# Attention between two feed-forward passes: the probability tile of each head's longest query tile transposed by DMA, and norm, loads and waits moved at the change of sequence

## Chip, cores and metric

One NeuronCore of a Trainium2 chip runs the whole program. The metric is the device time of one execution in microseconds (us); before the change it is 3945.35, the median of three runs (3943.01 to 3945.7). A difference of 0.2% is about 8 us.

## What is computed

`x` holds 8 sequences of 1024 tokens with 256 values each. Three stages follow one another, each with a layer norm ahead and a residual behind it:

```python
x = x + 0.5 * ffn(layernorm(x), w_gate, w_up, w_down)        # inputs and weights rounded blockwise to FP4
x = x + attention(layernorm(x), Wq, Wk, Wv, Wo, span_val)
x = x + 0.5 * ffn(layernorm(x), w_gate, w_up, w_down)
# attention: 16 heads of 64
w = einsum('bhqd,bhkd->bhqk', q, k) / 64 + causal            # -1e9 above the diagonal
w = softmax(w) * mask                                        # mask: one value per head and key
w = w / (sum(w) + 1e-8)
out = einsum('bhqk,bhkd->bhqd', w, v) @ Wo
```

Only the attention stage is touched, apart from the way the split weights are stored for it.

## The kernel before

**Pairs and visits.** The attention stage works on two heads at a time, a pair: 8 pairs per sequence, 64 in all. A pair goes through 16 *visits* (`UNITS`), one for each head and query tile of 128 rows, for each head in the order of tiles `ORDER = (7, 0, 5, 1, 6, 3, 4, 2)`. Because of the causal mask, tile j meets only the j+1 first key tiles. So visit 0 and visit 8 are the long ones: tile 7 of either head, 1024 keys wide.

**One visit.** TensorE computes the scores into one of two banks `s_ps` (L1121 to L1125). VectorE takes the row maximum (`at_neg_max`, L1298). ScalarE writes the exponentials to `at_e_rows`, with the row sum, which costs a second short instruction (L1215). The value product needs the keys on the partitions, so TensorE transposes `e_rows` in blocks of 128x128 float32 into one of two banks `t_ps` (L1135), in *groups* of up to four blocks (512 columns). ScalarE copies each group as the f16 high part (`at_eT_hi`, L1223), VectorE the f16 rest (`at_eT_lo`, L1304). TensorE multiplies both with the values into `o_ps` (L1149), ScalarE copies the result out (`at_o_raw`, L1231). There is one bank `o_ps`: the first product of a visit waits for the copy of the visit before.

**Side work.** Beside the visits runs the work for the next pair and the last one, in *pieces* that share one bank `at_side_ps`: two pieces each for q and k of the next pair, four for v of the next two pairs (in every second pair, called odd here; the others are the even ones), two transposes of the last pair's output (`o_turn`) and four products with Wo. A piece of q, k or `o_turn` is done when ScalarE has copied the high part (L1195) and VectorE the rest (L1266); only then may the next piece enter the bank. In the last pair of a sequence (the fresh pair) there are four more pieces that transpose the next sequence's normed input (`x_turn`).

**Order.** Every engine is in order. The order is written out by `pair_steps`, which gives TensorE, ScalarE and VectorE one list: scores run two visits ahead, a group's value product three groups behind its transposes (`LAG`), and a piece stands behind the group whose number `SLOTS` (or `FRESH_SLOTS`) names. The high and the low copy of a piece stand one place later in the list than the piece. The steps are `scores`, `turn` (transposes and high copy), `lo`, `max`, `value`, `copy`, `exp`, and the pieces. Semaphores carry the dependencies.

**Change of sequence.** The fresh pair begins on VectorE with the whole norm of the next sequence (`norm_x`: 8 statistics, 8 aggregations, a power on GpSimd, 8 normalisations) and TensorE's first `x_turn` waits for it. SyncE's queue issues all loads in program order: in the first pair of a sequence it loads the next x, stores the accumulator `at_acc` once the last products of the former sequence are added, loads it anew, and only then, in the next pair's part, loads `at_w_qk` for the pair after.

## Time and profile before

| | |
|---|---|
| median of three runs | 3945.35 us |
| the profiled execution | 3950.1 us, of which the span from first to last instruction 3948.3 us |
| mean granted TensorE clock | 0.962 of 2.4 GHz |
| busy share of the span | TensorE 89%, VectorE 76%, ScalarE 60%, GpSimd 21% |
| attention stage | about 600 to 3420 us of the span, 64 pairs |

How to read it: the busy shares are means over three stages. Inside the attention stage, the timeline rows have the start of an instruction in us from the span's start, its duration, the engine, the line of the kernel, the output and inputs, and the shapes. A matmul's duration is from start to finished result, and matmuls overlap; what one costs TensorE is the distance to the start of the next. In brackets stands how long the engine was idle before and what ended that.

### The profile page before, as it was taken

The numbers are of one execution on the slowest core, as the hardware profiler recorded it, in microseconds if no ns is written. First come the engines' busy times: TensorE is split into PE (matmuls) and PEld (weight loads), VectorE is DVE, ScalarE is ACT, GpSimd is POOL, SyncE is SP. The second block draws the span as 40 slices with busy tenths as digits, with TensorE's granted clock in tenths as the row PEclk, the third lists the DMA queues.
The fourth block names the chain that finished last, engine by engine and source line by source line (L and its number), as shares of the span: only waits on it lengthen the run. The fifth ranks groups of instructions, "written<-read, shape, count | busy, mean of one in ns | idle before, by whom it ended". The sixth has DMA issues, their size and how long they took to land. (4 is left out here: it accounts for less than half of the span.)

```text
span 3948.3 us, 90120 instructions
## 1 busy us (share of the span) xinstructions
PE 3531.2 (89%) x29924; PEld 3175.8 (80%) x29924; DVE 3005.0 (76%) x4884; ACT 2363.7 (60%) x5622; POOL 819.8 (21%) x830
## 2 busy tenths in 40 slices
PE   0899996998999899889988988998898899599998
PEld 0899995887787788778877877887787788499998
DVE  7899974777677677767766776777777677599996
ACT  1455543776676577667766766676676667445544
POOL 2232321111121121112111111121111112122332
PEclk6999998999999999999999999999999999799999
DMA  6111114533543444344444534353443534211110
GB/s 205 52 57 56 50 35 128 118 94 86 129 120 86 119 105 107 86 119 109 108 100 107 121 89 119 93 124 83 123 100 90 129 86 111 103 36 57 48 56 33
DMA packets 160297, 372.56 MB, mean 94 GB/s; under 512 B 19552, under 2 KB 59360, under 8 KB 159456
## 3 DMA queue, kind: packets, MB, share of 16 engines
q1 hardware_dynamic: 159968, 368.73, 36.1%
q8 instruction: 139, 2.28, 0.2%
q14 instruction: 190, 1.56, 0.1%
HBM read 128.79 MB, written 38.54 MB: 42 GB/s over the span
## 5 line engine op out<-in xcount | busy, mean ns | idle before, releaser
L1223 ACT ACTIVATE at_eT_hi<-at_t_ps 128x512 f16<-128x512 f32 (+3 forms) x1536 | 744.7, 491 | 565.5 <-PE at_t_ps L1135 520.3
L1304 DVE SCALAR_TENSOR_TENSOR at_eT_lo<-at_t_ps,at_eT_hi 128x512 f16<-128x512 f32 (+3 forms) x1536 | 824.7, 551 | 222.9 <-ACT at_eT_hi L1223 132.6
L1215 ACT ACTIVATE at_e_rows<-at_s_ps,at_neg_max 128x1024 f32<-128x1024 f32 (+7 forms) x1024 | 765.6, 748 | 111.0 <-DVE at_neg_max L1298 110.6
L1135 PE MATMUL at_t_ps<-at_ident,at_e_rows 128*128 128x128 f32 x4608 | 786.1, 280 | 33.0 <-DVE at_eT_lo L1304 29.2
L1298 DVE TENSOR_REDUCE at_neg_max<-at_s_ps 128x1 f32<-128x1024 f32 (+7 forms) x1024 | 766.5, 749 | 47.3 <-PE at_s_ps L1125 36.9
L1121 PE MATMUL at_s_ps<-at_kh_st,at_q_st 128*128 128x512 f32 (+2 forms) x1536 | 585.4, 381 | 54.6 <-ACT at_e_rows L1215 26.8
L1149 PE MATMUL at_o_ps<-at_v_cols,at_eT_hi 128*128 128x130 f16 x4608 | 611.2, 221 | 17.8 <-ACT at_o_raw L1231 16.2
L1149 PE MATMUL at_o_ps<-at_v_cols,at_eT_lo 128*128 128x65 f16 x4608 | 569.4, 193 | 0.0
L1135 PEld LDWEIGHTS at_t_ps<-at_ident,at_e_rows 128*128 128x128 f32 x4608 | 510.6, 142 | 70.3 <-DVE at_eT_lo L1304 46.9
L1122 PE MATMUL at_s_ps<-at_kl_st,at_q_st 128*128 128x512 f32 (+2 forms) x1536 | 518.3, 345 | 0.0
L1149 PEld LDWEIGHTS at_o_ps<-at_v_cols,at_eT_hi 128*128 128x128 f16 x4608 | 435.9, 98 | 34.4 <-ACT at_o_raw L1231 20.1
L1050 PE MATMUL at_side_ps<-at_xT_hi,at_w_qk 128*128 128x512 f32 x1012 | 390.8, 427 | 60.0 <-DMA at_w_qk<-w_qk_split 51.3
L1149 PEld LDWEIGHTS at_o_ps<-at_v_cols,at_eT_lo 128*128 128x128 f16 x4608 | 420.6, 98 | 16.7
L1121 PEld LDWEIGHTS at_s_ps<-at_kh_st,at_q_st 128*128 128x128 f32 x1536 | 293.3, 191 | 96.0 <-ACT at_e_rows L1215 38.7
L1014 POOL TENSOR_TENSOR at_o_sum<-at_o_raw 128x1040 f32<-128x1040 f32 x64 | 131.5, 2054 | 940.4 <-ACT at_o_raw L1231 940.4
L1122 PEld LDWEIGHTS at_s_ps<-at_kl_st,at_q_st 128*128 128x128 f32 x1536 | 294.8, 192 | 23.3
L425 POOL TENSOR_TENSOR ffn_h_q<-ffn_code,ffn_scale 128x704 f32<-128x704 f32 x128 | 175.4, 1391 | 585.8 <-DVE ffn_code L366 585.8
L1231 ACT ACTIVATE at_o_raw<-at_o_ps 128x130 f32<-128x130 f32 x1024 | 290.7, 284 | 2.1 <-PE at_o_ps L1149 1.6
L1050 PEld LDWEIGHTS at_side_ps<-at_xT_hi,at_w_qk 128*128 128x128 f32 x1012 | 196.6, 194 | 100.4 <-DMA at_w_qk<-w_qk_split 52.3
L530 PE MATMUL ffn_gu_ps<-ffn_w_gu_hi,ffn_xT_hi 128*128 128x352 f32 x1024 | 262.2, 337 | 14.5 <-DVE ffn_raw L329 10.0
L467 ACT ACTIVATE ffn_silu<-ffn_gu_ps 128x704 f32<-128x704 f32 x128 | 97.1, 759 | 282.6 <-PE ffn_gu_ps L530 282.6
L530 PE MATMUL ffn_gu_ps<-ffn_w_gu_lo,ffn_xT_hi 128*128 128x352 f32 x1024 | 250.4, 326 | 0.0
(184 smaller groups left out, 7402.2 us busy)
## 6 DMA issues: line engine op xcount, KB each, us to landing
at_kh_st<-at_k_hi SPq DMA_DIRECT2D x256, 256.0 KB, 4.4
at_kl_st<-at_k_lo SPq DMA_DIRECT2D x256, 256.0 KB, 5.8
at_w_qk<-w_qk_split SPq DMA_DIRECT2D x64, 512.0 KB, 6.1
at_q_st<-at_q_hi SPq DMA_DIRECT2D x128, 256.0 KB, 3.9
at_q_st<-at_q_lo SPq DMA_DIRECT2D x128, 256.0 KB, 4.9
at_w_v<-w_v_split SPq DMA_DIRECT2D x66, 256.0 KB, 5.7
at_w_out<-w_out_split SPq DMA_DIRECT2D x64, 256.0 KB, 5.7
ffn_x_rows<-in_L_attn_query_dram SPq DMA_DIRECT2D x32, 256.0 KB, 2.8
```

Source lines behind the costliest of these rows:

```text
L425: nc.gpsimd.tensor_tensor(blocks_of(h_q[:, par, j, :INNER]), blocks_of(code[:, j * INNER:(j + 1) * INNER]), per_block(scale[:, par, j * HB ...
L530: last = nc.tensor.matmul(gu_ps[:, c, 0:HALF_I], xT[a][:, par, kt, j * P:(j + 1) * P], gu[b][:, kt, c * HALF_I:(c + 1) * HALF_I], start=n ...
L1050: last = nc.tensor.matmul(bank[:], wts[:, w, s, kt, :], xT[t][:, kt, c * CHUNK:(c + 1) * CHUNK], start=i == 0, stop=i == len(passes) - 1)
L1121: nc.tensor.matmul(out, qs, kh_st[par][a][:, k0:k0 + w], start=True, stop=False)
L1122: last = nc.tensor.matmul(out, qs, kl_st[par][a][:, k0:k0 + w], start=False, stop=not lastc)
L1135: last = nc.tensor.transpose(t_ps[i % 2][:, b * P:(b + 1) * P], e_rows[:, n % 4, (k0 + b) * P:(k0 + b + 1) * P], ident[:])
L1149: last = nc.tensor.matmul(o_ps[:, :VPART[s]], eT[s][:, i % EBUF, b * P:(b + 1) * P], v_cols[par][:, k0 + b, a, :VPART[s]], start=k0 + b == ...
L1215: nc.scalar.activation(e_rows[:, n % 4, :w], s_ps[n % 2][:, col:col + w], ACT.Exp, bias=neg_max[:, n % 4:n % 4 + 1], accum_out=e_sum[:, pa ...
L1223: nc.scalar.activation(eT[0][:, i % EBUF, :count * P], t_ps[i % 2][:, :count * P], ACT.Copy, scale=PSCALE).then_inc(sem("eT_hi"), 1)
L1231: nc.scalar.activation(o_raw[:, a * QT + j, :], o_ps[:, :VCOLS], ACT.Copy).then_inc(sem("o_copied"), 1)
L1298: nc.vector.tensor_reduce(neg_max[:, n % 4:n % 4 + 1], s_ps[n % 2][:, col:col + P * (j + 1)], AX.X, ALU.max, negate=True).then_inc(sem("ma ...
L1304: nc.vector.scalar_tensor_tensor(out=eT[1][:, i % EBUF, :count * P], in0=t_ps[i % 2][:, :count * P], scalar=PSCALE, in1=eT[0][:, i % EBUF, ...
```

## The change

1. **Visits 0 and 8 (tile 7 of either head) get no `turn`.** Their two groups each leave the list `GROUPS` (24 groups become 20). Instead ScalarE copies the 1024 columns of `e_rows` as f16 high part into `e_flat` (`flat_hi`), right behind the visit's `exp`; VectorE writes the rest beside it (`flat_lo`), at the end of the visit before; SyncE issues one DMA transpose of 128 x 2048 f16 (512 KB) into `eT_flip`; and TensorE multiplies all eight blocks at once (`value_flip`), behind the last value group of the visit two further on (visit 2 or 10).
2. **The lists move**: `SLOTS`, `FRESH_SLOTS` and `NORM` are new, `max` stands at a visit's second place or where it has one only, `EBUF` is 5, the value product stays three groups behind, where groups are now fewer.
3. **Change of sequence**: `norm_x` goes in 14 steps into places 8 and up of the sequence's first pair, x is loaded at that pair's start, `at_w_qk` is loaded one pair earlier into the buffer that the pair has just used (two more pairs are stored in DRAM for that), and VectorE's wait for `at_acc` stands ahead of the first sum with Wo instead of at the pair's start.

```diff
+FLIPPED = (7,)
+FLIPS = [n for n, (a, j) in enumerate(UNITS) if j in FLIPPED]
+FLIP_AFTER = {n + 2: n for n in FLIPS}
-NORM = (7, 8)
-SLOTS = (0, 2, 4, 6, 8, 10, 11, 13, 15, 17, 19, 20, 21, 22)
+NORM = (6, 7)
+ROWS_FROM = 8
+SLOTS = (0, 1, 3, 5, 7, 9, 10, 11, 13, 15, 17, 18, 19, 20)
-EBUF = 6
+EBUF = 5
...
+    def values_of(i, dg):
+        steps.append(("value", i, dg))
+        m = GROUPS[i][0]
+        if LAST_GROUP[m] == i:
+            steps.append(("copy", m, dg))
+            if m in FLIP_AFTER:
+                steps.append(("value_flip", FLIP_AFTER[m], dg))
+                steps.append(("copy", FLIP_AFTER[m], dg))
...
-        for i in [i for i, (m, _, _) in enumerate(GROUPS) if m == n]:
-            first = GROUPS[i][1] == 0
+        for first, i in enumerate([i for i, (m, _, _) in enumerate(GROUPS) if m == n] or [None]):
+            place += 1
...
+            if rows and place >= ROWS_FROM:
+                steps.append(("norm_x", place - ROWS_FROM, 1))
...
+        if soon[0] in FLIPS and (soon[1] == 0 or after):
+            steps.append(("flat_lo",) + soon)
         if more:
             steps.append(("exp",) + unit)
+            if unit[0] in FLIPS:
+                steps.append(("flat_hi",) + unit)
...
+            def flip(f, g):
+                sp.wait_ge(sem("flat_lo"), g * len(FLIPS) + f + 1)
+                sp.sem_inc(sem("passed_sp"), 1)
+                sp.wait_ge(sem("value_done"), g * NV + (VALUES.index(("flip", FLIPS[f])) + 1 - NV + AHEAD["value_done"]))
+                sp.sem_inc(sem("passed_sp"), 1)
+                sp.dma_start_transpose(eT_flip[f][:], e_flat[f][:].rearrange("p s k -> p (s k)")).then_inc(sem(f"flipped{f}"), 16)
...
             def pair(b, r, par, before, after, fresh, twin):
                 g = b * PAIRS + r
+                flip(0, g)
+                if isinstance(r, int) and r == 0 and not (isinstance(b, int) and b == BATCH - 1):
+                    sp.wait_ge(sem("xn"), b * QT + QT)
+                    load_x(b + 1)
                 if after:
-                    if not (isinstance(g, int) and g == 0):
-                        sp.wait_ge(sem("k_done"), g * 2)
-                    load_qk(g + 1, 0 if fresh else r + 1, 1 - par)
+                    sp.wait_ge(sem("k_done"), g * 2 + 2)
+                    load_qk(r + 2, par)
                     place(g + 1, 1 - par)
+                flip(1, g)
...
+            def value_flip(n, g, par):
+                a, j = UNITS[n]
+                f = FLIPS.index(n)
+                pe.wait_ge(sem(f"flipped{f}"), g * 16 + 16)
+                pe.wait_ge(sem("o_copied"), g * NU + (COPIED.index(n) + AHEAD["o_copied"]))
+                for b in range(j + 1):
+                    for s in range(2):
+                        last = nc.tensor.matmul(o_ps[:, :VPART[s]], eT_flip[f][:, s * (j + 1) + b, :], v_cols[par][:, b, a, :VPART[s]],
+                                                start=b == 0 and s == 0, stop=b == j and s == 1)
+                last.then_inc(sem("value_done"), 1)
...
+            def flat_hi(n, g):
+                nc.scalar.activation(e_flat[f][:, 0, :], e_rows[:, n % 4, :w], ACT.Copy, scale=PSCALE).then_inc(sem("flat_hi"), 1)
...
+            def flat_lo(n, g):
+                nc.vector.scalar_tensor_tensor(out=e_flat[f][:, 1, :], in0=e_rows[:, n % 4, :w], scalar=PSCALE, in1=e_flat[f][:, 0, :],
+                                               op0=ALU.mult, op1=ALU.subtract).then_inc(sem("flat_lo"), 1)
```

What the list does to the engines is shown at three places. The lines of the changed kernel are numbered anew: L1181 is the old L1135 (transposes), L1195 the old L1149 (value products), L1167 to L1171 the scores.

**ScalarE, visit 7 to 8 of every pair.** Before, from visit 8's `exp` (1024 wide) to the high copy of the first `o_turn` piece and the first copy of a transposed group of visit 8:

```order
L1215 ACTIVATE at_e_rows,at_e_sum<-at_s_ps,at_neg_max 128x1024
...
L1223 ACTIVATE at_eT_hi<-at_t_ps 128x384
L1231 ACTIVATE at_o_raw<-at_o_ps 128x130
...
L1215 ACTIVATE at_e_rows,at_e_sum<-at_s_ps,at_neg_max 128x128
...
L1195 ACTIVATE at_oT_hi<-at_side_ps 128x512
...
L1223 ACTIVATE at_eT_hi<-at_t_ps 128x512
```

The same stretch now:

```order
L1278 ACTIVATE at_e_rows,at_e_sum<-at_s_ps,at_neg_max 128x1024
...
L1288 ACTIVATE at_e_flat<-at_e_rows 128x1024
...
L1296 ACTIVATE at_eT_hi<-at_t_ps 128x384
...
L1305 ACTIVATE at_o_raw<-at_o_ps 128x130
...
L1278 ACTIVATE at_e_rows,at_e_sum<-at_s_ps,at_neg_max 128x128
L1263 ISA
L1255 ACTIVATE at_oT_hi<-at_side_ps 128x512
L1278 ACTIVATE at_e_rows,at_e_sum<-at_s_ps,at_neg_max 128x768
L1255 ACTIVATE at_oT_hi<-at_side_ps 128x512
```

The copy to `e_flat` stands ahead of four instructions that other work waits for; the two 512-wide copies behind the first `oT_hi` are gone.

**TensorE, between the two `o_turn` pieces (visit 8).** Before, with repeated rows left out:

```order
L1089 MATMUL at_side_ps<-at_ident,at_o_norm 128x128 x4
...
L1125 MATMUL at_s_ps<-at_causal,at_ident_b 128x128
...
L1135 MATMUL at_t_ps<-at_ident,at_e_rows 128x128 x4
L1149 MATMUL at_o_ps<-at_v_cols,at_eT_hi 128x130
L1149 MATMUL at_o_ps<-at_v_cols,at_eT_lo 128x65
...
L1135 MATMUL at_t_ps<-at_ident,at_e_rows 128x128 x4
...
L1089 MATMUL at_side_ps<-at_ident,at_o_norm 128x128 x4
```

Now:

```order
L1135 MATMUL at_side_ps<-at_ident,at_o_norm 128x128 x4
...
L1167 MATMUL at_s_ps<-at_kh_st,at_q_st 128x512
L1168 MATMUL at_s_ps<-at_kl_st,at_q_st 128x512
L1167 MATMUL at_s_ps<-at_kh_st,at_q_st 128x256
L1168 MATMUL at_s_ps<-at_kl_st,at_q_st 128x256
L1171 MATMUL at_s_ps<-at_causal,at_ident_b 128x128
...
L1135 MATMUL at_side_ps<-at_ident,at_o_norm 128x128 x4
```

Between the two pieces only the scores are left; eight transposes and ten value products went (the products to later places).

**TensorE, between the two q pieces at a pair's start (visits 0 and 1).** Before, from the last product of the first q piece to the first of the second:

```order
L1050 MATMUL at_side_ps<-at_xT_hi,at_w_qk 128x512
...
L1135 MATMUL at_t_ps<-at_ident,at_e_rows 128x128 x4
...
L1149 MATMUL at_o_ps<-at_v_cols,at_eT_hi 128x130
L1149 MATMUL at_o_ps<-at_v_cols,at_eT_lo 128x65
...
L1125 MATMUL at_s_ps<-at_causal,at_ident_b 128x128
...
L1135 MATMUL at_t_ps<-at_ident,at_e_rows 128x128
```

Now:

```order
L1096 MATMUL at_side_ps<-at_xT_hi,at_w_qk 128x512
...
L1167 MATMUL at_s_ps<-at_kh_st,at_q_st 128x256
L1168 MATMUL at_s_ps<-at_kl_st,at_q_st 128x256
L1171 MATMUL at_s_ps<-at_causal,at_ident_b 128x128
L1179 ISA
L1181 MATMUL at_t_ps<-at_ident,at_e_rows 128x128
L1195 MATMUL at_o_ps<-at_v_cols,at_eT_hi 128x130
L1195 MATMUL at_o_ps<-at_v_cols,at_eT_lo 128x65
```

A group of four transposes and the products that stood with it are gone from here, and ahead of the first piece another group of four and eight products are gone; one run of eight products follows the single transpose.

## Rows read from the trace of the kernel before

**Rows 1.** Windows: us of the stretch, busy us of each engine (instructions), clock, DMA, GB/s
```profile
700.00:800.00 100.00, 97.07 (x911) 85.31 (x910) 78.30 (x137) 71.84 (x196) 19.37 (x22) 1.00 0.47 113
```
**Rows 2.** TensorE's waits, 800 to 3200 us: sum us, times, longest us
```profile
PE at_side_ps L1050 <- DMA at_w_qk<-w_qk_split: 51.3, 7, 7.9
PE at_side_ps L1081 <- DVE at_xn L1330: 41.2, 7, 5.9
```
**Rows 3.** Windows of 5 us behind either wait at one change of sequence
```profile
935.00:940.00 5.00, 5.00 (x37) 4.45 (x37) 3.04 (x6) 3.23 (x9) 2.05 (x1) 0.67 0.01 3
1030.00:1035.00 5.00, 5.00 (x25) 3.96 (x24) 2.14 (x4) 2.26 (x6) 0.00 (x0) 0.61 0.00 0
```
**Rows 4.** Timeline of TensorE, visit 6 of an even pair
```profile
742.97 0.61 PE L1135 MATMUL at_t_ps<-at_ident,at_e_rows 128*128 128x128 f32 x4
743.41 0.22 PE L1149 MATMUL at_o_ps<-at_v_cols,at_eT_hi 128*128 128x130 f16 x1
...
743.76 0.30 PE L1135 MATMUL at_t_ps<-at_ident,at_e_rows 128*128 128x128 f32 x1
```
**Rows 5.** Groups by shape, 700 to 800 us: busy us, mean ns
```profile
L1223 ACT ACTIVATE at_eT_hi<-at_t_ps 128x512 f16<-128x512 f32 x30 | 17.9, 597 | 14.9 <-PE at_t_ps L1135 12.6 <-issue 2.2
L1223 ACT ACTIVATE at_eT_hi<-at_t_ps 128x384 f16<-128x384 f32 x10 | 4.9, 489 | 3.2 <-PE at_t_ps L1135 2.9
L1298 DVE TENSOR_REDUCE at_neg_max<-at_s_ps 128x1 f32<-128x1024 f32 x5 | 6.1, 1224 | 0.5 <-PE at_s_ps L1125 0.2
```
**Rows 6.** Timeline of ScalarE, visits 7 and 8, same pair
```profile
744.54 1.11 ACT L1215 ACTIVATE at_e_rows<-at_s_ps,at_neg_max 128x1024 f32<-128x1024 f32 x1
...
746.02 0.27 ACT L1231 ACTIVATE at_o_raw<-at_o_ps 128x130 f32<-128x130 f32 x1
...
746.52 0.61 ACT L1195 ACTIVATE at_oT_hi<-at_side_ps 128x512 fp32r<-128x512 f32 x1
...
749.13 0.90 ACT L1215 ACTIVATE at_e_rows<-at_s_ps,at_neg_max 128x768 f32<-128x768 f32 x1
```
**Rows 7.** Timeline of VectorE, the same stretch
```profile
747.16 0.69 DVE L1266 SCALAR_TENSOR_TENSOR at_oT_lo<-at_side_ps,at_oT_hi 128x512 fp32r<-128x512 f32 x1 [0.45 <-ACT at_oT_hi L1195]
747.76 0.95 DVE L1298 TENSOR_REDUCE at_neg_max<-at_s_ps 128x1 f32<-128x768 f32 x1
```
**Rows 8.** Timeline of TensorE, the same stretch
```profile
747.02 0.61 PE L1135 MATMUL at_t_ps<-at_ident,at_e_rows 128*128 128x128 f32 x4
...
748.37 0.63 PE L1089 MATMUL at_side_ps<-at_ident,at_o_norm 128*128 128x128 f32 x4
...
750.18 0.50 PE L1121 MATMUL at_s_ps<-at_kh_st,at_q_st 128*128 128x512 f32 x1 [0.23 <-ACT at_e_rows L1215]
```
**Rows 9.** Timeline of ScalarE at visit 7 of the next, odd pair
```profile
785.39 0.49 ACT L1223 ACTIVATE at_eT_hi<-at_t_ps 128x384 f16<-128x384 f32 x1 [0.76 <-PE at_t_ps L1135]
```
**Rows 10.** Timeline of TensorE and ScalarE around the start of that pair
```profile
762.19 1.11 ACT L1215 ACTIVATE at_e_rows<-at_s_ps,at_neg_max 128x1024 f32<-128x1024 f32 x1
...
764.33 0.23 PE L1125 MATMUL at_s_ps<-at_causal,at_ident_b 128*128 128x128 bf16 x1
...
765.19 0.48 PE L1050 MATMUL at_side_ps<-at_xT_hi,at_w_qk 128*128 128x512 f32 x1
...
766.67 0.60 PE L1135 MATMUL at_t_ps<-at_ident,at_e_rows 128*128 128x128 f32 x4
...
768.59 0.48 PE L1050 MATMUL at_side_ps<-at_xT_hi,at_w_qk 128*128 128x512 f32 x1
```
**Rows 11.** Timeline of VectorE in the fresh pair: the normalisation
```profile
929.48 2.67 DVE L1330 TENSOR_SCALAR at_xn<-at_x,at_moments,at_rstd 128x256 f32<-128x256 f32 x8 [1.77 <-POOL at_rstd L983]
```
**Rows 12.** DMA of the page: packets, MB, share of 16 engines; KB and us to landing
```profile
q1 hardware_dynamic: 159968, 368.73, 36.1%
...
at_kl_st<-at_k_lo SPq DMA_DIRECT2D x256, 256.0 KB, 5.8
at_w_qk<-w_qk_split SPq DMA_DIRECT2D x64, 512.0 KB, 6.1
```
**Rows 13.** SyncE's queue in that even pair, last placements of k
```profile
744.09 3.39 SPq L913 DMA_DIRECT2D at_kl_st<-at_k_lo  x4
```

More of the change, by code:

```diff
@@ L608 @@
 LAG = 3
-EBUF = 6
+EBUF = 5
+VALUES, COPIED = [], []
+for group, (unit, _, _) in enumerate(GROUPS):
+    VALUES.append(("group", group))
+    if LAST_GROUP[unit] == group:
+        COPIED.append(unit)
+        if unit in FLIP_AFTER:
+            VALUES.append(("flip", FLIP_AFTER[unit]))
+            COPIED.append(FLIP_AFTER[unit])
+NV = len(VALUES)
 def score_chunks(j):
@@ L619, in score_chunks, with starts_rows, pair_steps @@
     return [(CHUNK - first, 0, first), (CHUNK, first, w - first)]
-def pair_steps(before, after, fresh, values):
+def starts_rows(b, r):
+    return isinstance(r, int) and r == 0 and not (isinstance(b, int) and b == BATCH - 1)
+def pair_steps(before, after, fresh, values, rows=False):
     q, k, v, turn_o, wo, turn_x = ([(kind, c, dg) for c in range(n)] for kind, n, dg in (
@@ L746, in stored @@
     def stored(sp):
-        for order, count in enumerate((128, 64, 64, 32)):
+        for order, count in enumerate((128, 128, 128, 32)):
             sp.wait_ge(sem(f"kept{order}"), count)
@@ L1167, in pair @@
                 prev = ("k_lo", 2 * g + 2)
-                for kind, i, dg in pair_steps(before, after, fresh, par == 1):
+                for kind, i, dg in pair_steps(before, after, fresh, par == 1, starts_rows(b, r)):
                     if kind == "scores":
@@ L1240, in pair @@
                 g = b * PAIRS + r
-                for kind, i, dg in pair_steps(before, after, fresh, par == 1):
+                for kind, i, dg in pair_steps(before, after, fresh, par == 1, starts_rows(b, r)):
                     if kind == "exp":
                         exp(i, g + dg, par ^ dg)
+                    elif kind == "flat_hi":
+                        flat_hi(i, g + dg)
                     elif kind == "turn":
```

145 lines of the change are left out of this document (84 added, 61 removed).

## The prediction, written before the changed kernel was run

> **What bounds the kernel now.** I read the windows first. In a stretch of the attention stage without a change of sequence TensorE is busy 97% at the full clock, VectorE 78%, ScalarE 72% [rows 1]: TensorE bounds it. Then its waits: apart from short ones there are two of 5.9 and 7.3 us, once per change of sequence [rows 2]: the first transpose of the new input waits for the norm, and a pair later the projection waits for its weights, which SyncE issues only after the accumulator's store and load. Behind either wait the granted clock is 0.67 and 0.61 for a while, between the levels 1.2 and 2.4 GHz, since TensorE had stood still [rows 3]. Last the timelines, for how much room TensorE's order leaves to the copies of the side bank. At visit 8 of an even pair the first `o_turn` piece's rest is done at 747.85 and TensorE asks for the bank at 748.37, 0.5 us later [rows 7, 8]: the pieces are spaced so that the transposes and products of the long visit just cover the copy chain.
>
> **The transposes that go.** Four transposes cost TensorE 0.44 us from start to start [rows 4]. Each flipped visit loses eight: 0.88 us, 128 times, 113 us. The 16 value products stay (four blocks 0.35, eight 0.70 us [rows 4]). ScalarE's two copies of 0.60 us become one of 1024 columns: 0.597 less 0.489 is 0.108 us per 128 columns, so 1.03 us [rows 5], and as with the others the next instruction starts some 0.1 us before its end: 0.9 us in the queue. Bounds: 0.5 (if the copy from SBUF ran at twice the rate) and 1.1 (the `exp` of that width [rows 6]). VectorE's `flat_lo`: nearest is the maximum over 1024 columns, 1.22 us [rows 5]; I take 1.2, bounds 0.6 and 1.3. As sums of busy time this is even; what matters is where they stand.
>
> **Visit 8, even pairs.** `flat_hi` stands right behind the `exp`, ahead of a copy, the next `exp` and the first `o_turn` piece's high copy. That copy started at 746.52 [rows 6]; now 747.43, done 748.03. The rest on VectorE follows (0.69 us): 748.75. TensorE has only the scores between the two pieces and asks for the bank at 747.02, where its four transposes started [rows 8]: it stands for 1.8 us. VectorE's maximum for visit 10 ends at 749.7, the `exp` (0.90 and the read of the sum) at 750.7, and the scores of visit 12, which wait for it, start 0.6 us later than the 750.18 of before [rows 8]. The 0.88 us saved are used up in that, and 0.35 us of products (visit 7's, before done by now) still have to be made. Two visits on, `value_flip` needs the copy of visit 10's result, which on ScalarE stands behind the high copy of the transposes just issued: 0.39 and 0.27 us [rows 5, 6] after those, while TensorE has 0.17 us of products: 0.8 us more. With 0.1 us of smaller waits for copies: **1.9 us lost** net of the saving.
>
> **Visit 8, odd pairs.** A v piece (1.5 us) stands ahead of visit 7's scores, and ScalarE waits for TensorE there, 0.76 us before it starts at 785.39 [rows 9]; `flat_hi` fits in. The chain ends as before, but TensorE still lacks work ahead of the second `o_turn` piece (0.9 us) and later for visit 12's `exp`, and the 0.35 and 0.8 us stand: **1.0 us lost**.
>
> **Visit 0.** The `exp` starts at 762.19 [rows 10], `flat_hi` ends at 764.3, `flat_lo` at 765.5; the maximum of visit 2 waited only for scores done at 764.56 [rows 10], and now for `flat_lo`. It ends at 766.4, its `exp` at 767.4, and only behind that comes the high copy of the first q piece, the rest at 768.7. TensorE has finished that piece (1.48 us) at 765.9 and has 0.88 us of work (two visits' remainders): it stands for 1.9 us and starts the second q piece at 768.72, against 768.59 [rows 10], the saving used up. Up to visit 7's scores three more things come: 0.35 us of products put off; visit 15's product waits for visit 14's copy, which stands behind a high copy (0.6 us); `value_flip` waits for visit 2's copy, behind the high copies of a k piece and of a group (0.9 us). Sum **2.0 us lost**. Where the pair before is odd, its v pieces cover `flat_hi` (ScalarE then waits for TensorE as in [rows 9]): **1.3 us**.
>
> **Sum of the flips.** An even and an odd pair together lose 1.9 + 1.0 + 2.0 + 1.3 = 6.2 us; 32 such: **+198**. If both new copies cost no time, each flip loses 0.9 less: +83. The transposes in the DMA queue I take as hidden; their price is a rival below.
>
> **The change of sequence.** The wait for weights goes: they are loaded a pair ahead, and the accumulator's wait stands at the first Wo sum, over half a pair later. The wait for the norm goes. 7 times 7.3 and 5.9 [rows 2] is 92 us. Of the reduced clock, windows at 0.67 and 0.61 lose 1.7 and 2.0 us of 5 [rows 3]: 4 us each time, 28 us. Together **-120**. Back comes: VectorE does the norm inside the sequence's first pair, eight normalisations of 2.67 us in all, as much for the statistics, and a wait of 1.77 us for GpSimd's power [rows 11], which blocks the row maxima queued behind it; most lies in VectorE's free 22%, I take 2 us; and with flipped visit 0 the short `x_turn` pieces have less work between them than q pieces, 2 us. 7 times 4: **+28**. Bounds 0 (all covered) and 60. The four extra stores of weights in front and the last pair's list are hidden or under 2 us.
>
> **Total.** 198 - 120 + 28 = 106 on the profiled execution's 3950.1 (span 3948.3 and 1.8 around it). The row-by-row chains leave out that one wait often absorbs the next; I take 15 us off for that, an estimate, and give **+90**. The profiled execution is 4.8 us above the median of 3945.35; on the median: **4035 us**. Ends: 83 - 120 = -37, 3908; and 198 - 120 + 60 and 15 for a longer `flat_lo`: 4100.
>
> **Rival 1: the saving stays (faster).** Mechanism: the high and low copies of four groups less in each pair let ScalarE and VectorE run ahead, so that `flat_hi` meets an idle engine everywhere, as in [rows 9], and the side bank is free in time. Then the 113 us go as well as the 120: 3945 - 113 - 120 + 28 = 3740; half of it gives 3850. It decides from less than 0.88 us of waiting per flip. For it: ScalarE is idle 28% [rows 1]. Against it: at visit 8 of the even pair the `o_turn` copy follows on ScalarE without a wait noted before it [rows 6], and the q chain is two copies long in any case (0.6 and 0.7 us) against 0.88 us of work.
>
> **Rival 2: the DMA transpose comes too late.** From `flat_lo` to `value_flip` are 14 us at visit 0, and 10 at visit 8, where the placements of k are still under way in the same queue: the last issue ends near 747.5 [rows 13] and lands 5.8 us later [rows 12], which leaves about 5.6 us in even and 8.6 in odd pairs. Bounds for the transpose: 6.1 us like the load of 512 KB; or, if it goes in rows of 256 bytes, 2048 packets at the mean 0.143 us per packet over 16 engines (0.361 x 3948.3 x 16 / 159968), 18.3 us [rows 12]. I take the load's value, with half of it overlapping the placements: hidden. At 10 us even pairs wait 2.4 us more, +77: 4110. At 18.3 it is some 13.5 us per pair, +860: 4900. The Trainium skill, "VectorE: DVE Perf Modes", section "The three transpose paths", gives 1309 ns for one 128x128 block by DMA against 390 on TensorE; 16 blocks one after the other would be 21 us, late at both visits. Its "DMA: Bandwidth & Descriptors", section "Latency and other measured facts", gives 261 GB/s, by which the 512 KB take 2 us. No row here shows a transpose; by the first page the time would be that of the 18.3 us case or above, by the second my sum stands.
>
> **Rival 3: only the clock and the change of sequence count.** If flips cost what they save: 3945 - 120 + 28 = 3853. It needs each flip to lose 1.6 us less than I read off; no row gives that.
>
> **Chances.** My forecast with its own range 3910 to 4110: 0.55. Rivals 1 and 3, 3740 to 3900: 0.28. Rival 2 at 4110 and above: 0.17. Range 3790 to 4200: it leaves out the lowest third of rivals 1 and 3 and half of rival 2. What a measurement tells from no change is 0.2%, 8 us. Faster by more: the 0.28 and 0.03 of my own low end, 0.31; within: 0.04; slower: 0.65.
>
> **What would show it.** Right: TensorE's busy share inside a sequence falls from 97 to some 90%, with waits of the side bank's pieces (L1096 for the second q piece, L1135 for `o_turn`) for `at_q_lo` and `at_oT_lo`, near 2 us each, and of the flipped products for `at_o_raw`; no wait for `at_w_qk` or `at_xn` in the middle; the copy to `e_flat` near 1.03 us, the rest 1.2; an even and an odd pair together 6 us longer than before. Wrong: pairs as long as before or shorter (rival 1 or 3), or flipped products that wait for the DMA (rival 2). A landing above 8 us for the transpose would refute that it is hidden.

## The result, and the profile after

The changed kernel takes 4110.2 us (median of 4 runs, 4108.7 to 4115.6) against 3945.5 us (4 runs, 3943.0 to 3946.2): a ratio of 1.042, 95% interval [1.040, 1.044], 165 us slower. The forecast was 4035 us, slower, with a range of 3790 to 4200: the direction and the range held, and the size was 75 us too small (90 us forecast, 165 measured).

One correction to the description of the order above: `max` stands at a visit's first place, as in the kernel before, not at its second.

The stretch of [rows 1] in the changed kernel (us of the stretch, busy us of each engine with instructions, clock, DMA, GB/s):

```profile
700.00:800.00 100.00, 85.98 (x785) 74.03 (x785) 69.82 (x117) 65.21 (x171) 20.61 (x20) 0.98 0.55 122
```

TensorE's share fell from 97 to 86%, and every other engine's but GpSimd's fell too: nothing else has become the bound, all of them wait for one another. TensorE's waits over the attention stage, 600 to 3580 us (sum us, times, longest us):

```profile
PE at_o_ps L1207 <- ACT at_o_raw L1305: 99.3, 128, 1.4
PE at_side_ps L1135 <- DVE at_oT_lo L1343: 96.5, 57, 2.3
PE at_side_ps L1096 <- DVE at_q_lo L1343: 84.1, 60, 2.3
PE at_o_ps L1195 <- ACT at_o_raw L1305: 41.5, 89, 0.7
PE at_t_ps L1181 <- DVE at_eT_lo L1381: 31.1, 67, 1.5
PE at_s_ps L1167 <- ACT at_e_rows L1278: 27.0, 52, 2.0
...
PE at_side_ps L1127 <- DVE at_xT_lo L1343: 23.8, 15, 2.5
```

The waits of [rows 2], for the weights and for the norm in mid-run, are gone. In their place stand the three that the prediction named: the flipped product (L1207) behind the copy of the last result, and the second piece of `o_turn` (L1135) and of q (L1096) behind VectorE's low copy. TensorE at visit 8 of an even pair, where [rows 8] had no wait at the second piece (start us, us, engine, line, operation; in brackets the idle time before it and its releaser):

```profile
754.23 0.63 PE L1135 MATMUL at_side_ps<-at_ident,at_o_norm 128*128 128x128 f32 x4
...
755.41 0.23 PE L1171 MATMUL at_s_ps<-at_causal,at_ident_b 128*128 128x128 bf16 x1
757.93 0.66 PE L1135 MATMUL at_side_ps<-at_ident,at_o_norm 128*128 128x128 f32 x4 [2.29 <-DVE at_oT_lo L1343]
...
759.81 0.80 PE L1167 MATMUL at_s_ps<-at_kh_st,at_q_st 128*128 128x512 f32 x1 [0.46 <-ACT at_e_rows L1278]
```

Between the two `o_turn` pieces TensorE has only visit 10's scores. ScalarE and VectorE at that place, to be read against [rows 6] and [rows 7]:

```profile
754.22 1.06 ACT L1288 ACTIVATE at_e_flat<-at_e_rows 128x1024 f16<-128x1024 f32 x1
755.19 0.47 ACT L1296 ACTIVATE at_eT_hi<-at_t_ps 128x384 f16<-128x384 f32 x1
...
755.72 0.37 ACT L1278 ACTIVATE at_e_rows<-at_s_ps,at_neg_max 128x128 f32<-128x128 f32 x1
...
756.06 0.60 ACT L1255 ACTIVATE at_oT_hi<-at_side_ps 128x512 fp32r<-128x512 f32 x1
```

```profile
755.32 1.95 DVE L1389 SCALAR_TENSOR_TENSOR at_e_flat<-at_e_rows,at_e_flat 128x1024 f16<-128x1024 f32 x1 [1.48 <-ACT at_e_flat L1288]
757.20 0.68 DVE L1343 SCALAR_TENSOR_TENSOR at_oT_lo<-at_side_ps,at_oT_hi 128x512 fp32r<-128x512 f32 x1
```

`at_oT_hi` stands behind the flat copy as the prediction had it, and was done at 756.66. The low copy did not follow it: VectorE was still writing the low half into the flat row, for 1.95 us instead of 1.2. That took the wait from the forecast 1.8 to 2.3 us (e6, below, takes GpSimd away from it and has 1.8).

The DMA rows that answer to [rows 12] (the page's queue row; then the transposes, what ended TensorE's idle time before the products that read them, and the transposes' landing, minimum, median and maximum):

```profile
q1 hardware_dynamic: 428528, 437.42, 44.5%
```

```profile
L965 SPq DMA_TRANSPOSE at_eT_flip<-at_e_flat x128: 1326/2626/6025, 649.1 to 3547.7; - x128
...
  ACT at_o_raw L1305: 99.3, 128
...
DMA to landing us min/median/max: 4.2/4.3/8.2
```

A transpose of 512 KB landed in 4.3 us, the slowest in 8.2. The 128 products that read one waited for ScalarE 128 times and for a DMA never: rival 2 is out.

### The profile page after: what moved, and what is told of

It reads as the page before. It is cut to its first block and busy times, and to the rows that moved or that the text cites. A ratio compares the mean times of both kernels' runs of the same rounds, so it can differ in the third digit from the quotient of the medians.

```text
span 4108.0 us, 88480 instructions
## 1 busy us (share of the span) xinstructions
PE 3456.1 (84%) x28900; PEld 3071.3 (75%) x28900; DVE 3018.8 (73%) x4756; ACT 2377.2 (58%) x5494; POOL 888.4 (22%) x830
## 5 line engine op out<-in xcount | busy, mean ns | idle before, releaser
L1296 ACT ACTIVATE at_eT_hi<-at_t_ps 128x512 f16<-128x512 f32 (+3 forms) x1280 | 588.2, 467 | 377.0 <-PE at_t_ps L1181 295.8
L1381 DVE SCALAR_TENSOR_TENSOR at_eT_lo<-at_t_ps,at_eT_hi 128x512 f16<-128x512 f32 (+3 forms) x1280 | 653.9, 523 | 85.9 <-ACT at_eT_hi L1296 78.6
L1181 PE MATMUL at_t_ps<-at_ident,at_e_rows 128*128 128x128 f32 x3584 | 622.3, 280 | 31.3 <-DVE at_eT_lo L1381 31.1
L1167 PE MATMUL at_s_ps<-at_kh_st,at_q_st 128*128 128x512 f32 (+2 forms) x1536 | 594.2, 387 | 56.6 <-ACT at_e_rows L1278 27.0
L1168 PE MATMUL at_s_ps<-at_kl_st,at_q_st 128*128 128x512 f32 (+2 forms) x1536 | 530.0, 352 | 0.0
L1195 PE MATMUL at_o_ps<-at_v_cols,at_eT_hi 128*128 128x130 f16 x3584 | 492.1, 223 | 41.7 <-ACT at_o_raw L1305 41.5
L1096 PE MATMUL at_side_ps<-at_xT_hi,at_w_qk 128*128 128x512 f32 x1012 | 386.9, 423 | 90.1 <-DVE at_q_lo L1343 84.1
L1195 PE MATMUL at_o_ps<-at_v_cols,at_eT_lo 128*128 128x65 f16 x3584 | 456.8, 194 | 0.0
L1181 PEld LDWEIGHTS at_t_ps<-at_ident,at_e_rows 128*128 128x128 f32 x3584 | 399.3, 143 | 49.2 <-DVE at_eT_lo L1381 35.7
L1195 PEld LDWEIGHTS at_o_ps<-at_v_cols,at_eT_hi 128*128 128x128 f16 x3584 | 344.5, 100 | 65.5 <-ACT at_o_raw L1305 40.0
L1167 PEld LDWEIGHTS at_s_ps<-at_kh_st,at_q_st 128*128 128x128 f32 x1536 | 299.9, 195 | 102.7 <-ACT at_e_rows L1278 40.6
L1195 PEld LDWEIGHTS at_o_ps<-at_v_cols,at_eT_lo 128*128 128x128 f16 x3584 | 331.2, 99 | 14.9
L1096 PEld LDWEIGHTS at_side_ps<-at_xT_hi,at_w_qk 128*128 128x128 f32 x1012 | 194.0, 192 | 136.3 <-DVE at_q_lo L1343 93.8
L1389 DVE SCALAR_TENSOR_TENSOR at_e_flat<-at_e_rows,at_e_flat 128x1024 f16<-128x1024 f32 x128 | 186.9, 1460 | 95.2 <-ACT at_e_flat L1288 91.8
```

Source lines behind the costliest of these rows:

```text
L1096: last = nc.tensor.matmul(bank[:], wts[:, w, s, kt, :], xT[t][:, kt, c * CHUNK:(c + 1) * CHUNK], start=i == 0, stop=i == len(passes) - 1)
L1167: nc.tensor.matmul(out, qs, kh_st[par][a][:, k0:k0 + w], start=True, stop=False)
L1168: last = nc.tensor.matmul(out, qs, kl_st[par][a][:, k0:k0 + w], start=False, stop=not lastc)
L1181: last = nc.tensor.transpose(t_ps[i % 2][:, b * P:(b + 1) * P], e_rows[:, n % 4, (k0 + b) * P:(k0 + b + 1) * P], ident[:])
L1195: last = nc.tensor.matmul(o_ps[:, :VPART[s]], eT[s][:, i % EBUF, b * P:(b + 1) * P], v_cols[par][:, k0 + b, a, :VPART[s]], start=k0 + b == ...
L1296: nc.scalar.activation(eT[0][:, i % EBUF, :count * P], t_ps[i % 2][:, :count * P], ACT.Copy, scale=PSCALE).then_inc(sem("eT_hi"), 1)
```

## The experiments

All kernels start from the changed kernel unless said otherwise; times are medians of 4 runs each.

**e1, only the moves at the change of sequence.** No visit is flipped, and the places are those of the kernel before.

```
-FLIPPED = (7,)
+FLIPPED = ()
-EBUF = 5
+EBUF = 6
(SLOTS, FRESH_SLOTS and NORM as before; calls of flip, flat_hi and flat_lo left out)
```

> The changed kernel without flips: all visits are transposed on TensorE with the lists of before, but the norm in steps, the earlier weight load and the later wait for the accumulator stay. My account: a change of sequence saves 15 us (from the pair times of the two traces), so about 3945 - 105 = 3840, and the flips alone then cost 4110 - 3840 = 270, 2.1 us each. Rival A (the moves bring less, most of the loss is at the change of sequence): about 3900 or above. Rival B (the moves bring the full 120 forecast, nothing comes back): 3825.

Measured 3855.2 us (3853.9 to 3859.6), ratio to before 0.977 [0.975, 0.979]. The stretch without a change of sequence and the waits over 800 to 3200 us, as in [rows 1] and [rows 2]:

```profile
700.00:800.00 100.00, 96.96 (x913) 85.22 (x913) 78.64 (x139) 72.34 (x198) 19.49 (x22) 1.00 0.48 114
```

```profile
PE at_t_ps L1179 <- DVE at_eT_lo L1378: 43.0, 97, 1.2
...
PE at_side_ps L1125 <- DVE at_xT_lo L1340: 12.2, 14, 0.9
```

The moves alone save 93 us; that is between the expected 105 and rival A. So the flips, together with the lists that came with them (`SLOTS`, `FRESH_SLOTS`, `NORM`, `EBUF`), cost 4110 - 3855 = 255 us. This is the fastest kernel of the study and beats both.

**e10 and e11, one flip alone.** Only visit 0, or only visit 8, goes by DMA; the other's two groups stay on TensorE with the places of before.

```
-FLIPS = [n for n, (a, j) in enumerate(UNITS) if j in FLIPPED]
+FLIPS = [0]     (e11: [8])
-SLOTS = (0, 1, 3, 5, 7, 9, 10, 11, 13, 15, 17, 18, 19, 20)
+SLOTS = (0, 1, 3, 5, 7, 9, 10, 12, 14, 16, 18, 19, 20, 21)     (e11: (0, 2, 4, 6, 8, 10, 11, 12, 14, ...))
-EBUF = 5
+EBUF = 6
(GROUPS, the calls of flip, FRESH_SLOTS and, in e11, NORM to match)
```

> Only visit 0 goes by the DMA transpose; visit 8 keeps its two groups on TensorE, and the side bank's pieces stand one place per place as in the kernel before from there on. All else as in the changed kernel (its moves at the change of sequence too, which alone gave 3855 us). Theory (each flip has its own price, from the waits right behind it, nearly independent): visit 0's waits are the q_lo wait (84 us over the run) and half the o_raw waits of the product, and visit 8's the oT_lo wait (97 us), the clock behind it and the other half, so this kernel stands 45 to 50 percent of the 255 us above 3855: 3955 to 3990 us, with the oT_lo wait near none and the q_lo wait near 84 us. Rival (the loss comes from what two flips leave together, too few instructions between the recurrences of a whole pair): well under half of the cost, below 3930 us.

> Only visit 8 goes by the DMA transpose; visit 0 keeps its two groups on TensorE, with the pieces of the first half where the kernel before has them. Theory (each flip has its own price): the oT_lo wait of about 97 us stays, the clock falls behind it as in the changed kernel, the q_lo wait goes: 50 to 55 percent of 255 us above 3855, 3975 to 4000 us; this and the kernel with only visit 0 together lose 255 us, within 25. Rival (loss from the two together): both under 3930 us, together far less than 255. A third, that GpSimd's stretch of VectorE's copy (1.95 us here against 1.22 at visit 0) carries the difference between the two flips: this one at least 40 us above the other.

Measured: visit 0 alone 3997.4 us (3989.9 to 3998.7), ratio 1.012 [1.011, 1.014]; visit 8 alone 3974.0 us (3972.4 to 3978.9), ratio 1.007 [1.005, 1.009]. Above e1 that is 142 and 119 us, together 261 against 255 for both: the two prices add up. (Either kernel lies a few us outside the range expected for it, e10 above, e11 below.) Both have `EBUF` at 6, so the 5 of the changed kernel is not what costs it time. e10 and e11, waits over 600 to 3580 us:

```profile
PE at_side_ps L1095 <- DVE at_q_lo L1343: 84.9, 63, 2.2
PE at_o_ps L1206 <- ACT at_o_raw L1305: 52.1, 64, 0.8
```

```profile
PE at_side_ps L1134 <- DVE at_oT_lo L1342: 80.9, 57, 1.8
PE at_o_ps L1206 <- ACT at_o_raw L1305: 47.1, 64, 1.3
PE at_s_ps L1166 <- ACT at_e_rows L1277: 41.5, 94, 2.0
```

Each kernel keeps its own piece's wait and half of the product's. Visit 0 is the dearer one, so visit 8 is not dearer by 40 us. But e11 doesn't test what GpSimd does: in it VectorE's copy took 1.22 us in the even pairs and 1.57 us at most, never 1.95, and the second `o_turn` piece waited 1.8 us. That question is e6's.

**e7, both copies cut to 128 columns.** The rest of the flat rows stays zero, which leaves most of the longest tile's probabilities out of the products.

```
-activation(e_flat[f][:, 0, :], e_rows[:, n % 4, :w], ...)
+activation(e_flat[f][:, 0, :P], e_rows[:, n % 4, :P], ...)     (flat_lo the same)
```

> The changed kernel with both copies of a flipped visit cut from 1024 to 128 columns; the rest of at_e_flat is zero, so this leaves part of the probabilities out; transposes by DMA and products are whole. My account (of the 255 us that flips cost against moves alone, 0.9 us or more per flip comes from the length of the copies in the chains, the rest from the thin order and the waits for at_o_raw): time falls by 110 to 190 us, to 3920 to 4000, still 65 to 145 above the 3855 of the moves alone. Rival A (the copies are the whole loss): 3860 or below. Rival B (the order alone costs it, the copies are hidden): within 40 us of 4110.

Measured 4035.2 us (4032.7 to 4042.2), ratio 1.023 [1.021, 1.024]: 75 us less, under the 110 that were expected at least: the 896 columns taken off either copy are worth a good quarter of the 255 us. The `oT_lo` wait fell from 96.5 to 52.7 us, but the `q_lo` wait only to 78.9 and the product's stayed at 99.3. ScalarE at the start of the pair behind an even one shows why, first in e7, then in the kernel before:

```profile
775.65 0.21 ACT L1278 ACTIVATION_READ_ACCUMULATOR at_e_rows<-at_s_ps,at_neg_max 128x1 f32 x1
778.10 0.90 ACT L1278 ACTIVATE at_e_rows<-at_s_ps,at_neg_max 128x768 f32<-128x768 f32 x1 [2.24 <-PE at_t_ps L1181]
...
779.00 0.59 ACT L1255 ACTIVATE at_q_hi<-at_side_ps 128x512 fp32r<-128x512 f32 x1
```

```profile
764.08 0.21 ACT L1215 ACTIVATION_READ_ACCUMULATOR at_e_rows<-at_s_ps,at_neg_max 128x1 f32 x1
766.52 0.60 ACT L1223 ACTIVATE at_eT_hi<-at_t_ps 128x512 f16<-128x512 f32 x1 [2.23 <-issue]
```

The maximum that the exponentials need had ended at 776.80, and no semaphore of this `exp` hangs on a transpose of the new pair, so the releaser in the row is not the reason. The same 2.2 us stand in the kernel before, where they are put down to "issue". Over the stage each of these two is one row of ScalarE's waits (before, then e7):

```profile
ACT at_eT_hi L1223 <- issue: 36.9, 16, 2.5
```

```profile
ACT at_e_rows L1278 <- PE at_t_ps L1181: 34.4, 16, 2.3
```

16 times is 8 sequences by the two jumps back of the three-fold loop over pairs (L919), and in either trace they come in twos, one turn of the loop apart. That it is the jump follows from this place and count; what in it takes the time is open. Before, TensorE's first q piece and a group's transposes hid this; with visit 0 flipped it is laid bare once the copies no longer cover it. At most other pair starts e7 still waits 1.14 us for `q_lo`, with the short flat copies done in time: scores, maximum (0.95), `exp` (0.90 and 0.2), high copy (0.6) and low copy (0.7) are 3.3 us one after the other, and TensorE has about 2.4 us of work beside them.

**e2, the pieces spread out again** (not in the fresh pairs).

```
-SLOTS = (0, 1, 3, 5, 7, 9, 10, 11, 13, 15, 17, 18, 19, 20)
+SLOTS = (0, 2, 4, 6, 7, 9, 10, 12, 14, 15, 17, 18, 19, 20)
```

> The changed kernel with five side pieces one place later (second q piece 1 to 2, k pieces 3 to 4 and 5 to 6, second o_turn piece 11 to 12, first Wo product 13 to 14); same work. My account (TensorE stands for the side bank because too little work lies between two pieces): the waits for at_q_lo (84 us) and at_oT_lo (97 us) fall below 30 each, the clock no longer falls at visit 8, and the time falls by 130 to 200 us, to 3910 to 3980. Rival (ScalarE's and VectorE's queues are the limit, TensorE only waits elsewhere): the waits move to the scores (for the exp) and the time falls by under 60 us, to 4050 or above.

Measured 4038.6 us (4037.0 to 4039.4), ratio 1.023 [1.021, 1.025]: 72 us less, the most of any repair, but under the 130 expected (and over the rival's 60). Its waits over 600 to 3580 us:

```profile
PE at_s_ps L1167 <- ACT at_e_rows L1278: 112.1, 126, 2.0
PE at_o_ps L1207 <- ACT at_o_raw L1305: 100.5, 128, 1.4
...
PE at_side_ps L1135 <- DVE at_oT_lo L1343: 15.9, 57, 1.5
```

The waits for `q_lo` and `oT_lo`, 181 us, fell to 30 (14.5 and 15.9), and 85 us came back at the scores, which wait for the exponentials of two visits before. With the side bank free in time, the next recurrence binds.

**e12, the side bank's copies ahead of the exponentials.** TensorE's order is the same.

```
+        if n in (0, 7):
+            flush(late_hi)
+            flush(late_lo)
         if soon[0] in FLIPS and (soon[1] == 0 or after):
             steps.append(("flat_lo",) + soon)
```

> The changed kernel with one difference in the order of ScalarE and VectorE at visits 0 and 7: the two copies of the side bank's piece (q at visit 0, the first o_turn piece at visit 7) stand ahead of the exponentials of the next visit but one and ahead of the low copy into the flat rows, not behind them. TensorE's order is the same. Theory (the waits for q_lo and oT_lo are chains of five instructions in the queues of ScalarE and VectorE, flat copy, maximum, exponentials, high copy, low copy, of which only the last two belong to the bank): the q_lo wait of 84 us falls under 35, since the first q piece's copies can then start when TensorE ends it, and the oT_lo wait of 97 us under 60; of these some 100 us a part comes back, because the maximum and the exponentials stand later: 4110 - 50 to - 90, 4020 to 4060 us. Rival (TensorE's order is too thin there whatever the other engines do first, each wait that goes is waited at the next scores): under 25 us gained, 4085 us or more, with 90 us or more for the exponentials at the scores.

Measured 4098.2 us (4097.6 to 4102.6), ratio 1.039 [1.037, 1.040]: only 12 us less, the rival. The waits over 600 to 3580 us:

```profile
PE at_s_ps L1170 <- ACT at_e_rows L1281: 99.5, 70, 2.0
PE at_o_ps L1210 <- ACT at_o_raw L1308: 99.3, 128, 1.4
PE at_side_ps L1138 <- DVE at_oT_lo L1346: 61.4, 57, 1.5
PE at_side_ps L1099 <- DVE at_q_lo L1346: 45.6, 62, 1.3
```

The two piece waits fell by 74 us, the scores' wait rose by 72: whichever of the two chains goes first, TensorE stands for the other.

**e3, filler work before the second `o_turn` piece of even pairs.** Eight matmuls of 512 columns, whose result nothing reads.

```
+                pe.wait_ge(sem("eT_lo"), ...)           (its bank is free)
+                for _ in range(8):
+                    nc.tensor.matmul(t_ps[0][:], ...)     (512 columns, ahead of ("o_turn", 1))
```

> The changed kernel with eight matmuls of 512 columns (about 1.8 us, their result is overwritten unread) put into TensorE's wait ahead of the second o_turn piece in even pairs. My account (in even pairs the wait of 2.3 us lets the clock fall to 0.5 for 3.5 us behind it): the clock stays at 1.00 there, the wait itself shrinks to 0.5 us and the time falls by about 32 times 1.6 us, 50 us, to 4060. Rival (the low clock is incidental, only the wait counts): 4110 or, if the filler delays the piece, up to 4130.

Measured 4109.8 us (4105.2 to 4112.9), ratio 1.041 [1.039, 1.043]: no change, as the rival had it. TensorE can do 32 times that work for nothing, so the place is bound by the copies. The `oT_lo` wait fell from 96.5 to 37.3 us, taken up by the filler.

**e4, the flipped product behind the place's piece.** One more thing differs: the second k piece stands one place later, in the product's place.

```
-SLOTS = (0, 1, 3, 5, 7, ...)
+SLOTS = (0, 1, 3, 6, 7, ...)
...
-                steps.append(("value_flip", FLIP_AFTER[m], dg))
-                steps.append(("copy", FLIP_AFTER[m], dg))
+                held.append(("value_flip", FLIP_AFTER[m], dg))     (flushed after the piece)
+                held.append(("copy", FLIP_AFTER[m], dg))
```

> The changed kernel with each flipped product behind the side piece of its place instead of ahead of it, and the second k piece in that place too; same work. My account (0.8 us of waiting for at_o_raw at each of 128 flipped products because nothing lies between the copy and the product): this wait falls from 99 us to under 15 and the time by 70 to 100 us, to 4010 to 4040. Rival (the wait is slack that another wait takes over, the exp of two visits on being late): under 30 us, 4080 or above.

Measured 4105.6 us (4104.2 to 4107.2), ratio 1.040 [1.038, 1.042]: 5 us less, the rival. The product's wait, the largest of all, fell from 99.3 to 10.9 us and gave nothing: other waits, for `at_eT_lo` (31 to 54 us) and a new one for `at_k_lo` (31 us), took most of its place. The last is the edit's own: it stands at the first v piece, which now follows the moved k piece directly. So the 5 us are not the pure price of the product's wait; what its removal gives by itself was not run.

**e5, both flat copies one visit later, and e6, GpSimd held until VectorE's flat copy has ended.**

```
 e5:
-            steps.append(("flat_lo",) + soon)     (n + 1)
+            steps.append(("flat_lo", n, 0))       (and flat_hi of n + 1 in place of n + 2)
 e6:
+                    pool.wait_ge(sem("flat_lo"), g * 2)     (ahead of GpSimd's writes of v_cols and the mask)
```

> The changed kernel with both copies of a flipped visit one visit later in the lists: the high copy behind the next visit's exp, the rest at the end of the flipped visit itself instead of ahead of it; same work. My account (the copies stand ahead of the o_turn and q chains and lengthen them by 0.9 to 2 us): the waits for at_oT_lo (93 us) and at_q_lo (84 us) fall together by 60 to 110 us and the time by 50 to 100, to 4010 to 4060; the transposes still land in time. Rival (the order of the copies does not matter, since the same ScalarE and VectorE work precedes the next exp anyway): within 15 us of 4110.

> The changed kernel with GpSimd waiting for visit 8's rest (at_e_flat on VectorE) before it writes the next pair's values; same work. My account (VectorE's write of at_e_flat takes 1.96 us in even and 1.54 in odd pairs beside GpSimd's copies and 1.22 without, and in even pairs this pushes TensorE's wait from the forecast 1.8 to 2.3 us, behind which the clock falls): all of these writes take 1.22 us, the wait for at_oT_lo falls from 93 to about 65 us, the clock stays up at visit 8, and the time falls by 32 times 1 to 2.3 us, 30 to 75 us, to 4035 to 4080. Rival (GpSimd is unrelated, or the clock falls after 1.6 us of waiting just as well): under 25 us.

Measured: e5 4092.6 us (4090.3 to 4095.8), ratio 1.037 [1.035, 1.039], 18 us less; e6 4103.1 us (4102.4 to 4111.4), ratio 1.040 [1.039, 1.042], 7 us less, with runs that overlap those of the changed kernel. Neither gives the 50 and 30 us expected at least. In e5 the two piece waits stayed (99.0 and 78.5 us, from 96.5 and 84.1), against the account on which it rested. In e6 VectorE's copy takes what it takes at visit 0 and the second `o_turn` piece waits 1.81 us, the forecast 1.8:

```profile
755.87 1.23 DVE L1392 SCALAR_TENSOR_TENSOR at_e_flat<-at_e_rows,at_e_flat 128x1024 f16<-128x1024 f32 x1 [1.47 <-ACT at_e_flat L1291]
757.25 0.69 DVE L1346 SCALAR_TENSOR_TENSOR at_oT_lo<-at_side_ps,at_oT_hi 128x512 fp32r<-128x512 f32 x1 [0.16 <-ACT at_oT_hi L1258]
```

The collision was real, and worth at most some 7 us of 255.

**e8, four repairs together.** The edits of e4, e5 and e6 with `SLOTS = (0, 2, 4, 6, 8, 9, 10, 12, 14, 15, 17, 18, 19, 20)`.

> The changed kernel with four repairs at once: the side bank's pieces spread over later places, the DMA-fed value product behind the place's piece, both copies into the flat rows one visit later, and GpSimd held off its next writes until VectorE's copy of visit 8 has ended. Alone three of these gave 4.7 us (product behind the piece), 17.8 us (copies later) and 7.3 us (GpSimd held), and the pieces 71.8 us. Theory (each wait is a separate price): their sum, 4110 - 102 = about 4010 us, 3980 to 4040; VectorE's q_lo and oT_lo waits under 20 us together and the o_raw wait of the product under 20 us. Rival (the waits only move between one bank's recurrence and the next, because TensorE has nothing else to fill them with): 4030 to 4060 us, with the exponentials' wait of the scores at 90 us or more. A second rival, that the flips pay once their neighbours are out of the way: under 3855 us.

Measured 4074.4 us (4071.3 to 4078.3), ratio 1.032 [1.031, 1.034]. Theory and rivals missed: the sum of the single gains is 102 us, together they give 36, and e2's pieces alone were faster. The rival (4030 to 4060 us) was nearest, and its sign, 90 us of waiting for the exponentials, is there. The waits are spread over many small ones:

```profile
PE at_s_ps L1172 <- ACT at_e_rows L1283: 89.5, 76, 2.0
PE at_t_ps L1186 <- DVE at_eT_lo L1386: 54.7, 99, 1.4
...
PE at_side_ps L1113 <- DVE at_v_masked L1362: 33.6, 61, 0.8
```

Its clock is the poorest of all. I sum TensorE's busy time times one minus the granted clock over windows of 1 us, 650 to 3590 us: e1 loses 15 us, e7 37, e3 43, e2 and e5 44 each, the changed kernel 67, e8 93. This is read from one execution of each kernel. The mean clock of a kernel's executions scatters: from 0.961 to 0.973 in the kernel before, whose times lie within 7 us, and a hundredth of its span is 39 us. Differences of these sums are rough.

**e9, a second transpose of half the size ahead of each.** It goes into rows that nothing reads.

```
+                sp.dma_start_transpose(eT_spare[:], e_flat[f][:, 0, :]).then_inc(sem("spare"), 16)
                 sp.dma_start_transpose(eT_flip[f][:], ...)
```

> The changed kernel with a second DMA transpose of half the size (the high half, 256 KB) issued ahead of each of the 128, into rows that nothing reads. Theory (the transposes are hidden: landed in 4.3 us and needed a visit and more later): within 10 us of the changed kernel, 4100 to 4120 us, no wait of the DMA-fed product for a DMA. Rival (the queues or the DMA engines are near what they can give, and a longer transpose makes the product or the next loads late): over 20 us slower, 4130 us or more, with the value product of the last visit waiting for its DMA.

Measured 4129.0 us (4127.1 to 4130.0), ratio 1.046 [1.045, 1.048]: 19 us more, between the theory's 10 and the rival's 20. No product waited for a DMA, and the rows of TensorE's waits agree with the changed kernel's to 5 us each; 7 us of the 19 may be clock. Where the rest is I could not read off. A transpose is hidden but perhaps not quite free: no run takes away the 128 of the changed kernel while keeping all else.

## Why the prediction was right in direction and too small in size

**The change of sequence: right.** Forecast -120 + 28 = -92; e1 gives 3948.0 - 3855.2 = 93 us. It holds no flips, so of the +28 the 14 for the thin `x_turn` pieces should not be in it, and the forecast for e1 alone would be -106, 13 us too much.

**The parts of the 75 us.** The flips were put at 198 us and cost 255, which is 57. The discount for waits that absorb each other was 15. The rest is 3 us: the change of sequence and the medians.

**The sizes of the operations: right.** The high flat copy took 1.06 us (forecast 1.03), the low one 1.22 at visit 0 (forecast 1.2). At visit 8 it took 1.95 in the even pairs and 1.5 in most odd ones, beside GpSimd: not foreseen, and small (e6).

**The row-by-row chains: right to 0.3 us where nothing disturbed them.** Forecast and measured: second `o_turn` piece 1.8 and 2.29 us in even pairs (1.81 in e6), 0.9 and 1.01 in odd; second q piece of an odd pair 1.9 and 2.20 (1.6 in the first odd pair of a sequence); visit 15's product 0.6 and 0.60; flipped products 0.9 and 0.83, 0.8 and 0.67. Chains laid by hand from durations and order alone come that near to single waits. The start of an even pair has a wait for `q_lo` too, 1.18 us, to which the forecast gave no figure of its own.

**The sum of the flips: 198 forecast, 255 measured.** Per even and odd pair visit 0 was to lose 2.0 + 1.3 = 3.3 us and lost 142 / 32 = 4.4; visit 8 2.9 and lost 119 / 32 = 3.7. The mechanism stands, and both terms are too small. One cost that neither holds is the granted clock, which I had counted as a gain at the change of sequence and not as a cost of the new waits. Behind the 2.3 us wait at visit 8 of the next even pair (847 to 852 us; the row of 850 reads 0.50 as that of 849):

```profile
847.00:848.00 1.00, 0.60 (x5) 0.60 (x6) 1.00 (x2) 0.00 (x0) 0.00 (x0) 1.00 1.07 213
848.00:849.00 1.00, 1.00 (x12) 0.89 (x11) 0.67 (x2) 0.76 (x1) 0.00 (x0) 0.56 1.11 167
849.00:850.00 1.00, 1.00 (x7) 0.74 (x5) 0.25 (x1) 0.89 (x4) 0.00 (x0) 0.50 1.22 220
...
851.00:852.00 1.00, 1.00 (x9) 0.99 (x9) 0.68 (x1) 0.43 (x3) 0.00 (x0) 0.74 0.73 199
```

0.50 is the lower level, 1.2 GHz, and this fall costs 0.44 + 0.50 + 0.50 + 0.26 = 1.7 us. Over the stage the changed kernel loses 67 us to the clock and e1 15: 52 us that the flips bring, and that their terms lacked. This is of the size of the missing 57, but that it is the cause is not shown, since sums from one execution are rough, and the runs disagree. For it is e5: its waits for ScalarE and VectorE in the rows of over 9 us are as in the changed kernel (453 and 452 us), its clock loses 24 us less, and it is 18 us faster. Against it is e3: the loss fell by 24 us and the time did not, 15 us of it coming back as waits for the exponentials and for `at_o_raw`. A count from e1 to the changed kernel comes near the whole: TensorE's waits for ScalarE and VectorE (the rows of over 9 us, 600 to 3580 us) rise from 144 to 452 us, the transposes save 113, the clock loses 52, which is 308 - 113 + 52 = 247 of 255.

**The 15 us for waits that absorb each other: wrong way.** For removals the opposite of a discount holds: two flips add up (142 + 119 against 255), and a repaired wait comes back as another. e4 removed 88 us of waits (and made 31 of its own) and gained 5, e12 74 and 12, e2 150 and 72. What absorbs is the repair, not the damage. The forecast gave no row for this term.

**The low end, 3908 with free copies: wrong.** The copies look rightly priced: 0.9 us per flip, of which e7's copies of 0.31 us keep about 0.3, would be 77, and e7 gained 75. In part that is luck, since the price was meant as waiting alone: from the changed kernel to e7 the waits in the rows of over 9 us fall by 46 us, and the other 31 are clock. Wrong was what would be left. By the forecast e7 should stand 198 - 77 = 121 us above e1; it stands 180 above. The gap of 59 us is the missing 57 over again, so it does not lie in the length of the copies. Without any copy some 140 us would be left (255 - 115, an estimate), not 83. My reading of the rest is that it is what the flip takes from TensorE: the 0.88 us of transposes were the cover of two chains (scores to exponentials, side bank to its low copy) and, at visit 0, of ScalarE's 2.2 us at the loop's jump. e2 and e12, in which one chain's wait returns as the other's, bear it out, and in e7 taking the transposes off is no saving even with copies of an eighth. Two parts of the lists were not run apart: the lag of three groups between transposes and products, and how far behind its visit the flipped product stands.

**The rivals.** Rivals 1 and 3 (3740 to 3853) are out: each flip loses time (e10, e11); that e1 stands at 3855 is the change of sequence, not flips that cost nothing. Rival 2 is out by the landings. Its sums had a step that the text does not give: 10 us against the 5.6 left in even pairs is 4.4 us, not 2.4, and 18.3 us gives 15.5 us per pair, not 13.5; 2 us per visit 8 were taken off. Rival 2 was also backed by the Trainium skill, "VectorE: DVE Perf Modes", section "The three transpose paths", with 1309 ns per block. By that figure 16 blocks one after the other would be 21 us, an estimate; the trace, which decides, has 4.3 us for the whole transfer. The 2 us that the prediction has beside it are too short as well. My 18.3 us for 2048 packets at the queue's mean had the count about right and the packet wrong: against e1 (162288 packets, 37.2% of a span of 3853.5) the queue has 266,240 packets more, 2080 per transpose, and they hold (0.445 x 4108.0 - 0.372 x 3853.5) x 16 = 6310 us of DMA engine time, 0.024 us each instead of 0.143.

## What to carry to other kernels

Work taken off the engine that bounds a kernel can be worth less than nothing while that work is the cover of a chain through the other engines: before moving it, lay the chain from row durations and count what the bounding engine still has to do between asking for a buffer and getting it. Look at the granted clock behind each new wait of about 2 us; here it fell at one place and held at another. And when a change bundles a gain with a loss, run each part alone first: here the moves at the change of sequence were worth 93 us and the flips cost 255.
